# bo as a product on TensorE, the probability's exponent from its maxima on ScalarE, and narrow VectorE operations with one SBUF operand

## The reference

```
x = x + linear_attention(layernorm(x))   # 16 heads of 16, causal, elu+1 features
        values = (q . running sum of k v^T) / (q . running sum of k + 1e-6)
        return values @ Wo + bo
x = x + moe(layernorm(x))                # 8 experts, 2 per token
        logits = x @ router_w^T;  top 2;  p = softmax of the two
        out = sum over the two experts of p * (gelu(x @ w1^T + b1) @ w2^T + b2)
```

## Time and profile before

| | |
|---|---|
| median of 3 runs | 1074.2 us (1073.3 to 1074.75) |
| profiled execution, its own time | 1070.12 us |
| its span | 1068.0 us |
| PE busy | 941.2 us, 88% of the span |
| DVE busy | 835.4 us, 78% |
| ACT busy | 657.2 us, 62% |
| POOL busy | 670.5 us, 63% |
| granted TensorE clock, mean | 0.966 of full |

### The profile page before, as it was taken

The page is one execution under the profiler, slowest core; times in us unless marked ns, Lnnn a source line. Parts: engine busy times, 40 slices in busy tenths (PEclk is TensorE's granted clock), DMA queues, the critical chain, the costliest instruction groups (busy, mean ns, idle before and its releaser), DMA issues.

```text
span 1068.0 us, 31902 instructions
## 1 busy us (share of the span) xinstructions
PE 941.2 (88%) x10010; PEld 771.1 (72%) x10011; DVE 835.4 (78%) x2220; ACT 657.2 (62%) x1248; POOL 670.5 (63%) x580
## 2 busy tenths in 40 slices
PE   6789889988898898899888925899999999999995
PEld 3467667766776676677667723678999999999994
DVE  5779999999999999999998775456666666666663
ACT  8667776777677767767775332445555555555552
POOL 2226587787778777877878452356656656555665
PEclk9899999999999999999999856999999999999998
DMA  5916956546655664566455282355555565555554
GB/s 156 214 58 169 256 145 169 149 138 172 159 123 157 160 174 117 157 170 144 140 154 141 87 313 73 62 81 84 99 93 90 94 98 87 93 98 90 89 98 49
DMA packets 127242, 138.84 MB, mean 130 GB/s; under 512 B 12400, under 2 KB 120304, under 8 KB 126512
## 3 DMA queue, kind: packets, MB, share of 16 engines
q1 hardware_dynamic: 100288, 101.45, 38.1%
q0 software_dynamic: 25680, 35.01, 17.9%
q10 hardware_dynamic: 1184, 1.18, 0.4%
HBM read 71.08 MB, written 66.53 MB: 129 GB/s over the span
## 4 chain that ended last, share of the span: by engine, by line
PE 42%; DVE 35%; issue 8%; DMA 6%; ACT 3%; POOL 3%; SPq 1%; POOLq 0%; DVEq 0%; ACTq 0%
PE pF L488 9%; DVE ahl L1132 8%; PE pS L488 8%; PE pU L488 7%; PE pA L488 4%; DVE xn L1145 4%; PE pO L488 4%; DMA out<-yt,to_token 3%; DVE xn L1233 2%; PE pO L594 2%; DVE pd L1216 2%; DVE st L1111 2%; DVE w1s L1252 2%; ACT ahl L875 2%; DVE v L1192 2%
## 5 line engine op out<-in xcount | busy, mean ns | idle before, releaser
L1680 POOL DMA_INDIRECT out<-yt,to_token x135 | 218.1, 1615 | 178.5 <-DVE yt L1528 90.8
L875 ACT ACTIVATE ahl<-pS 128x512 f16<-128x512 f32 x240 | 141.0, 599 | 82.5 <-PE pS L573 80.9
L1132 DVE SCALAR_TENSOR_TENSOR ahl<-pS,ahl 128x512 f16<-128x512 f32 x240 | 160.8, 680 | 19.8 <-ACT ahl L875 19.4
L1581 POOL DMA_INDIRECT expert_in<-xn,cur x128 | 129.1, 1009 | 35.1 <-issue 33.4
L570 PE MATMUL pS<-cbs 128*128 128x512 bf16 x240 | 92.8, 387 | 23.8 <-DVE ahl L1132 19.9
L1055 ACT ACTIVATE g<-pS,b1s 128x256 f32<-128x256 f32 (+1 forms) x140 | 57.3, 462 | 87.9 <-PE pS L488 87.9
L1494 DVE TENSOR_TENSOR ghl<-g,ghl 128x1024 f16<-128x1024 f32 (+1 forms) x68 | 83.0, 1220 | 20.9 <-ACT ghl L1080 20.9
L488 PE MATMUL pS<-gT,w1s 128*128 128x256 f16 (+1 forms) x840 | 96.4, 271 | 1.0 <-DVE gT L1489 0.9
L488 PE MATMUL pF<-w2s,ghl 128*128 x816 | 95.1, 273 | 2.0 <-issue 1.1
L1539 POOL TENSOR_TENSOR rs<-ve,cfs 128x4 f32<-128x4 f32 x31 | 32.2, 1040 | 102.3 <-DVE ve L1102 102.3
L488 PE MATMUL pF<-xT,was 128*128 128x512 f16 x384 | 93.0, 379 | 3.1 <-DVE xT L1137 2.5
(11 more groups left out here) (193 smaller groups left out, 2293.0 us busy)
## 6 DMA issues: line engine op xcount, KB each, us to landing
xg<-expert_in SPq DMA_DIRECT2D x64, 260.0 KB, 3.1
qk_parts<-qkhl SPq DMA_DIRECT2D x32, 512.0 KB, 2.9
qst<-qk_parts SPq DMA_DIRECT2D x96, 128.0 KB
kst<-qk_parts SPq DMA_DIRECT2D x48, 256.0 KB
xs<-x SPq DMA_DIRECT2D x16, 512.0 KB, 5.4
xr<-x SPq DMA_DIRECT2D x16, 512.0 KB, 4.9
out<-x SPq DMA_DIRECT2D x16, 512.0 KB, 3.2
expert_in<-pads SPq DMA_DIRECT2D x16, 260.0 KB, 3.9
```

Of the source, the lines that this page charges most:

```text
L875: nc.scalar.activation(ahl[:, b % 2, 0, n * 4 * C:(n + 1) * 4 * C], score_bank(fr, n)[:], ACT.Relu).then_inc(sc_hi, 1)
L1132: V.scalar_tensor_tensor(ahl[:, b % 2, 1, cols], score_bank(fr, n)[:], 0.0, ahl[:, b % 2, 0, cols], ALU.max, ALU.subtract).then_inc(sc_lo, 1)
L1581: G.indirect_dma_start(xg_dram, bass.IndirectOffsetOnAxis(ap=cur[:, qp, 2 * b + t:2 * b + t + 1], axis=0), xn2[:, qp, b], None).then_inc(s ...
L1680: G.indirect_dma_start(out, bass.IndirectOffsetOnAxis(ap=to_token[:, c % 2, s:s + 1], axis=0), yt[:, c % 2, s], None, compute_op=ALU.add). ...
```

## The change

Four things change:

1. bo no longer goes through POOL. It is kept as two fp16 parts in boh (BR is 32; rows 0 to 31 the high part of bo*16/32, rows 32 to 63 the rest), made once in the prologue by one ACT and one DVE operation. out_project begins with a product of 64 rows of ones with boh, and the 6 products add to it. add_bo is gone, and DVE's residual waits for the load of xr itself, which has a semaphore for each of its two buffers.
2. The gap pd (L1216) is gone. ACT takes exp(m1 - m0) for each b by itself, with m1 as the bias and -1 as the scale: four operations of 128x1 where one of 128x4 was.
3. ixf and pos lie in PSUM (in pR), cnt and the second probability are made by tensor_reduce over one operand, and the first expert's column is written in the router and not in row_data.
4. w1_low stands behind norm1_stats, some five operations later.

The diff, cut to its core:

```diff
-        bos = sb("bos", [P, D], F32, att)
+        boh = sb("boh", [2 * BR, D], F16, att)
+        bos = at
+        ixf = pR[:, 336:336 + 2 * B].rearrange("p (b t) -> p b t", b=B)
+        pos = pR[:, 352:352 + B * E].rearrange("p (b e) -> p b e", b=B)
...
@@ SP
-                    sp.dma_start(xr[:, par], x_steps[bass.ds(i, 1)].rearrange("i p b d -> p (i b) d")).then_inc(xr_in, 16)
+                    sp.dma_start(xr[:, par], x_steps[bass.ds(i, 1)].rearrange("i p b d -> p (i b) d")).then_inc(xr_in[par], 16)
...
@@ PE, split3 and out_project
-                    mm = nc.tensor.matmul(out, lhs(a, k), rhs(b_, k), start=(t == 0), stop=(t == len(terms) - 1))
+                    mm = nc.tensor.matmul(out, lhs(a, k), rhs(b_, k), start=(t == 0 and not go_on), stop=(t == len(terms) - 1))
...
+                    if first_s and b == 0:
+                        pe.wait_ge(bo_lo, 1)
+                    nc.tensor.matmul(pA[:, D:2 * D], chs[0:2 * BR, H_ONES:H_ONES + P], boh[:], start=True, stop=False)
-                    split3(pA[:, D:2 * D], lambda a, k: aT[:, a, k], lambda a, k: was[:, a, 3, k], KC).then_inc(wo_ps, 1)
+                    split3(pA[:, D:2 * D], lambda a, k: aT[:, a, k], lambda a, k: was[:, a, 3, k], KC, go_on=True).then_inc(wo_ps, 1)
...
@@ ACT, prologue and sc
+                    nc.scalar.activation(boh[:], bos[0:2 * BR], ACT.Copy, scale=WS / BR).then_inc(bo_hi, 1)
-                    act.wait_ge(top_gap, q + 1)
-                    nc.scalar.activation(one_exp[:, :, 1], pd[:, 0], ACT.Exp).then_inc(top_exp, 1)
+                    act.wait_ge(rt, RT * q + 2)
+                    for b in range(B):
+                        nc.scalar.activation(one_exp[:, b, 1:2], mx[:, b, 0:1], ACT.Exp, bias=mx[:, b, 1:2], scale=-1.0).then_inc(top_exp, 1)
...
@@ DVE, residual
-                        dve.wait_ge(xr_done, s + 1)
+                        dve.wait_ge(xr_in[s_par], 16 * (s_half + 1))
@@ DVE, router
-                    V.scalar_tensor_tensor(pd[:, 0], mx[:, :, 1], 1.0, mx[:, :, 0], ALU.mult, ALU.subtract).then_inc(top_gap, 1)
...
-                    V.tensor_tensor(cnt[:], oh[:, :, 0], oh[:, :, 1], ALU.add).then_inc(cnt_done, 1)
+                    V.tensor_reduce(xn2[:, rp, :, FIRST], ixf[:, :, 0:1], AX.X, ALU.add).then_inc(rt, 1)
+                    with nc.allow_low_precision("0 or 1"):
+                        V.tensor_reduce(cnt[:], oh[:].rearrange("p b t e -> p b e t"), AX.X, ALU.add).then_inc(cnt_done, 1)
@@ DVE, row_data
-                    V.tensor_reduce(xn2[:, qp, :, FIRST], ixf[:, :, 0:1], AX.X, ALU.add)
-                    dve.wait_ge(top_exp, q + 1)
+                    dve.wait_ge(top_exp, 4 * q + 4)
-                    V.scalar_tensor_tensor(xn2[:, qp, :, PROB2], pd[:, 2], 1.0, one_exp[:, :, 1], ALU.mult, ALU.mult)
+                    V.tensor_reduce(xn2[:, qp, :, PROB2], one_exp[:, :, 1:3], AX.X, ALU.mult)
@@ DVE, body, c == 0
+                        dve.wait_ge(bo_hi, 1)
+                        V.scalar_tensor_tensor(boh[BR:2 * BR], bos[BR:2 * BR], WS / BR, boh[BR:2 * BR], ALU.mult, ALU.subtract).then_inc(bo_lo, 1)
...
                 if bk:
                     residual(s, 0, sp_)
-                if fr and c >= 2:
-                    w1_low()
...
                     norm1_stats(i + 1)
+                if fr and c >= 2:
+                    w1_low()
...
@@ POOL
-            def add_bo(i, c):
-                pool.wait_ge(xr_in, 16 * i + 16)
-                G.tensor_tensor(xr[:, c % 2], xr[:, c % 2], bos[:].unsqueeze(1).to_broadcast([P, B, D]), ALU.add).then_inc(xr_done, 1)
-                        add_bo(0, 0)
-                        add_bo(1, 1)
-                if fr and c >= 2:
-                    add_bo(i, c)
```

More of the change, by code:

```diff
@@ L59 @@
 C_TOKEN, C_END = C_PAD + PADS, C_PAD + PADS + STEPS * B
+BR = 32
 H_TRI, H_ONES, H_END = 0, 128, 256
@@ L159, in build @@
         ix = sb("ix", [P, B, 8], U32, att)
-        ixf = sb("ixf", [P, B, 2], F32, att)
-        pd = sb("pd", [P, 3, B], F32, att)
-        one_exp = sb("one_exp", [P, B, 2], F32, att)
+        pd = sb("pd", [P, B], F32, att)
+        one_exp = sb("one_exp", [P, B, 3], F32, att)
         oh = sb("oh", [P, B, 2, E], F32, att)
@@ L165, in build @@
         base = sb("base", [P, E], F32, att)
-        pos = sb("pos", [P, B, E], F32, att)
         sel = sb("sel", [P, B, 2, E], F32, att)
@@ L257, in build @@
         TAB = 30
-        RT = 10
+        RT = 11
         def front_of(j, c):
@@ L481, in _, with split3 @@
         def _(pe):
-            def split3(out, lhs, rhs, n, parts=((0, 0), (0, 1), (1, 0)), low_wait=None):
+            def split3(out, lhs, rhs, n, parts=((0, 0), (0, 1), (1, 0)), low_wait=None, go_on=False):
                 terms = [(a, b_, k) for a, b_ in parts for k in range(n)]
@@ L1215, in router @@
                         ins = V.max_index(ix[:, b], mx[:, b], lg[:, b])
-                    V.scalar_tensor_tensor(pd[:, 0], mx[:, :, 1], 1.0, mx[:, :, 0], ALU.mult, ALU.subtract).then_inc(top_gap, 1)
                     link(r, ins)
-                    link(r, V.tensor_reduce(ixf[:], ix[:, :, 0:2].unsqueeze(3), AX.X, ALU.add))
+                    link(r, V.tensor_reduce(ixf, ix[:, :, 0:2].unsqueeze(3), AX.X, ALU.add))
                     link(r, V.tensor_tensor(oh[:].rearrange("p b t e -> p (b t) e"),
@@ L1220, in router @@
                                             cfs[:, C_IOTA8:C_IOTA8 + E].unsqueeze(1).to_broadcast([P, 2 * B, E]),
-                                            ixf[:].rearrange("p b t -> p (b t)").unsqueeze(2).to_broadcast([P, 2 * B, E]), ALU.is_equal))
-                    V.tensor_tensor(cnt[:], oh[:, :, 0], oh[:, :, 1], ALU.add).then_inc(cnt_done, 1)
+                                            ixf.rearrange("p b t -> p (b t)").unsqueeze(2).to_broadcast([P, 2 * B, E]), ALU.is_equal))
+                    V.tensor_reduce(xn2[:, rp, :, FIRST], ixf[:, :, 0:1], AX.X, ALU.add).then_inc(rt, 1)
@@ L1238, in router_slots @@
                         dve.wait_ge(base_set, 1)
-                    link(q, V.tensor_tensor(pos[:], pR[:, POS:POS + B * E].rearrange("p (b e) -> p b e", b=B),
+                    link(q, V.tensor_tensor(pos, pR[:, POS:POS + B * E].rearrange("p (b e) -> p b e", b=B),
                                             base[:].unsqueeze(1).to_broadcast([P, B, E]), ALU.add))
-                    link(q, V.tensor_tensor(sel[:], oh[:], pos[:].unsqueeze(2).to_broadcast([P, B, 2, E]), ALU.mult))
+                    link(q, V.tensor_tensor(sel[:], oh[:], pos.unsqueeze(2).to_broadcast([P, B, 2, E]), ALU.mult))
                     if c >= 5:
```

14 lines of the change are left out of this document (8 added, 6 removed).

## The result

| | before | changed |
|---|---|---|
| median of the runs | 1073.95 us (4 runs, 1073.3 to 1074.75) | 1126.01 us (4 runs, 1122.99 to 1131.35) |
| profiled run, its span | 1070.1, 1068.0 us | 1131.35, 1129.6 us |
| mean granted clock of the span | 0.966 | 0.920 |

The ratio is 1.049 [1.0468, 1.0513]: slower by 5%, where 1036 us and faster had been forecast. The experiments showed later that this sign belongs to some chips; on another the same kernel took 0.977 of before. The trace of the run above is read first.

A forecast was written before the change was run, and what follows sets the result against it. DVE looked like the bound, but its stalls behind POOL made PE wait. Twelve steps 35, step 3 1.5, prologue 2.0, less drain 0.9, make 37.6 us off 1074.2: 1036 us, range 1024 to 1051, chance 0.62.

The forecast's parts named there:

- PE 32.69 + 0.44 + the kept wait: Attention step: PE's busy time, four bo products and the remaining wait make 33.9 us, against 36.82 before.
- the kept wait: PE's wait for the rest of aT behind the two norm2_apply: 0.8 of 0.94 us a step stays.
- a falling clock: PE's granted clock, 1.00 before, falling in the denser steps; named as making the forecast wrong, without size or chance.
- The stalls: Narrow two-SBUF-operand DVE operations held by long POOL operations: removing pd's and the second probability's ends PE waits of 1.67 and 1.07 us.
- D: Rival: stalls move to another two-operand operation, norm2_apply or w1_low, with like gain and loss; no change; chance 0.02.
- A: Rival: the q and k trip through DRAM limits the step to 35.2 us; 22 us gained, 1052 us; chance 0.17.
- B: Rival: PE alone bounds the step, all waits go, norm2_apply's too: 33.1 us a step, 1027 us; chance 0.15.
- step 3's 1.5: In attention step 3, losing the 2.07 us stall of oh gains 1.5 us.
- the drain's 0.9: In the drain, 8 more products lose 0.9 us.
- The prologue: Before the steps, removing add_bo frees DVE's feature(0) and the chain to the w1raw load: 2.0 us gained.
- The four exponents: On ACT, three more exponents cost 0.3 to 0.6 us; 0.4 us lateness for q and k parts, none on PE.
- Rival C: One-operand narrow DVE operations also stand behind POOL, while products cost more than waits return: 1080 us, slower; chance 0.04.
- product at a whole record: Upper bound for each bo product on PE: 0.27 us without overlap, 1.1 us a step.

The follow-up runs named there:

- S: Group of chips, not a run: those where the kernel before takes 1074 to 1076 us; the first result's chip is counted to it.
- F: Group of two chips, not a run: those where the kernel before takes 1065 to 1066 us.
- e1: The changed kernel without the product of bo, POOL adding bo again, on S: 1057.8 us, 0.985 of before.
- e9: The changed kernel itself, unaltered, on F: 1041.9 us, 0.977 of before.
- e18: The changed kernel without the product of bo and without add_bo, so bo is added nowhere, on F: 1031.5 us, 0.967 of before.
- e5: The changed kernel with the product of bo over 128 rows instead of 64, on F: 1034.3 us, 0.970 of before.
- e16: The changed kernel without the product of bo, POOL adding bo again; e1 repeated on another chip of S: 1056.1 us, 0.981 of before.
- e11: The changed kernel without the product of bo, POOL adding bo again; e1's kernel on F: 1100.5 us, 1.035 of before.
- e10: The changed kernel with the product of bo over 128 rows; e5's kernel again on F, beside e9: 1037.4 us, 0.974 of before.

## Why the prediction was wrong

**The failed step** is the sum "PE 32.69 + 0.44 + the kept wait" at a clock of 1.00: it took every completion of PE to be seen as promptly as before, and named a falling clock only as what would make it wrong. On S completions came late twice a step, 2.1 us behind attend(2) and 2.9 to 5.0 us behind attend(3), and the clock fell once a step: 40.33 us instead of 33.9. Against the step of the same kernel on F (33.98) that is 6.35 us more. 3.02 of them are idle time of PE (3.96 against 0.94): the waits of 0.35 and 0.64 us behind attend(2), and the pauses in attend(3). The other 3.33 are busy time (36.37 against 33.04 for 405 and 404 operations), which is what the lower clock costs. That the lateness brings the pauses, and the pauses the fall of the clock, is argued from their order in time and not shown; e1 shows only that the lateness behind attend(2) isn't enough. Nothing in the trace of before shows a late completion or hints at one; as its chip isn't known, it doesn't tell whether before has them on S.

**Why they come** is not settled. Shown: they are there on all three S chips in every kernel traced there (all have the row-data and router edits, or the product), and not in any trace on F, nor in the one trace of before. Those behind attend(3), and with them the clock's fall, come where the product is in and add_bo out (1.024 to 1.085), not where add_bo is back (0.981 to 0.985). Whether the product or POOL's freed time brings them is open: no kernel traced on S had both product and add_bo, or neither. Load of the DMA engines alone is not it: the pauses in attend(3) stand where the DMA share is 1.03 (219 to 225), but on F it is 1.07 over the same operations (e9, 172 to 178), without lateness, and behind attend(2) it was 0.17 (216 to 217). What differs between the chips isn't known. On F the changed kernel itself ran on one chip; its variants with the product did too, and e18, without it, on the second.

**The step on F** came out at 33.98 us against 33.9, with PE's busy time (33.04 against 33.13) and the kept wait (0.94 against 0.8) as summed. The stalls went as claimed, and D is excluded. (Of its readings one was loose: pd ended 0.03 us behind POOL's operation and the second probability 0.10, where the text says some 0.1 for both.) A, the late kst, took 3.1 us in three of twelve steps. B can't be, since the wait for aT stayed in every step. So the mechanism of the step was right on F, where completions are prompt. The gain of the whole was smaller than summed, as follows.

**The total on F.** The sum gave a span of 1068.0 - 37.6 = 1030.4 us; e9's is 1034.9. Cut as above, e9 is 71.8 + 446.7 + 516.4, the sum 69.1 + 441.7 + 519.6 (two of the 37.6 us fall ahead, step 3's 1.5 and eleven steps' 2.9 in the middle, step 15's 2.9 less the drain's 0.9 behind). The prologue gave nothing: add_bo went, but ACT's exponents pace qf there, and the load of w1raw starts at 48.07 instead of 47.75 us. The 13 steps are 34.4 us each on average, not 34.0, with the waits for kst in some. The part behind the steps is 3 us shorter than summed, which no term of mine explains; this is a chip where before is 8 us faster too, and it has no trace of before. So the gain there is 24 us (1041.9 against 1065.8), and not 37.6.

The price of the product, by PE's rows of e9 (64 rows) and e5 (128 rows):

```profile
165.61 0.38 PE L575 MATMUL pS<-qst,kst 96*128 96x256 f16 x2
165.93 0.28 PE L624 MATMUL pA<-boh,chs 64*128 64x256 f16 x1
166.14 0.83 PE L490 MATMUL pA<-was,aT 128*128 128x256 f16 x6
```

```profile
166.09 0.38 PE L575 MATMUL pS<-qst,kst 96*128 96x256 f16 x2
166.31 0.27 PE L624 MATMUL pA<-boh,chs 128*128 128x256 f16 x1
166.42 0.82 PE L490 MATMUL pA<-was,aT 128*128 128x256 f16 x6
```

From the scores to split3 it is 0.53 us with 64 rows, 0.33 with 128 and 0.23 without a product (e18, 163.43 to 163.66). So at this place it costs 0.30 and 0.10 us, where I took 0.11 for the 64-row one. Over a step less of it is left: the step without its waits is 33.04 us in e9, 32.67 in e5 (33.81 - 0.94 - 0.20) and 32.57 in e18 (33.67 - 0.94 - 0.16), one step read in each. The four cost 0.47 us together against the 0.44 of the sum.

**The four exponents.** The issue time of the four on ACT, from the start of the first to what follows:

```profile
191.32 0.88 ACT L959 ACTIVATE one_exp<-mx 128x1 f32<-128x1 f32 x4
192.06 0.66 ACT L936 ACTIVATE w1s<-w1raw 128x512 f16<-128x512 f32 x1
```

0.74 us for four, against 0.10 for one: 0.64 more, just over my 0.3 to 0.6. The estimate from the figures of the Trainium skill, page "ScalarE: Activation LUTs", section "What ACT_TABLE_LOAD costs", was 0.75, and the trace agrees. On F none of PE's waits is for ACT, so none of it was on PE's path.

**Rival C** had the sign on S and none of its mechanism: no one-operand form stands, and its "product at a whole record" (0.27 us) is near what the 64-row product costs at one place, yet four of them are not the 3.5 us a step that were lost.

## What to carry to other kernels

- A forecast that fills the last pauses of PE should hold a case in which PE's clock or its reports don't follow, with a chance of its own; here all that was slower had 4% together. One stable time on one chip is no evidence for another: the same two kernels change places here.
- Measure the kernels to be compared beside each other on one chip. Four runs on a new chip looked like proof that 128 rows cure what they don't.
- In this kernel VectorE's operations with two SBUF operands were cheap only where GpSimd paused when they arrived (1.89 us for two in e16, 4.15 in e11). If you take work off GpSimd, look there first.
- The product that adds the constant row was better over all 128 rows than over 64: 0.10 against 0.30 us at one place, and 14 us of the whole on S. On F it was 4.6 us between medians, with intervals that overlap (e10 and e9).

## What the runs showed of the hardware

- Completions of TensorE can reach the other engines late, while its own rows go on: 1.7 to 2.3 us behind attend(2), 2.1 to 5.4 behind attend(3) (in the changed kernel VectorE's waits for them are 1.5 to 3.7 us each, 50.3 in 405), once or twice per step, at the same places in every step, on three chips; no trace of the two others has them.
- The clock fell to the lower level once a step inside a stretch of pauses: in attend(3) on S after waits of 0.35 and 0.64 us and pauses of 0.16 and up to 0.54, in e11 some 1.3 us into a wait of 3.06. Before waits 1.67 and 1.07 us in each step at 1.00.
- The fastest kernel that computes the whole is the one with 128 rows, on F: 0.970 [0.9675, 0.973]. On S it is e1's: 0.981 [0.9771, 0.9855]. No kernel that ran on both groups beats before on both.
